# Causal attention by a second score product with keys on the partitions, in place of turned probabilities

## What is computed

```python
q, k = _apply_rope(q, k, cos, sin)          # q, k, v: (8, 16, 512, 8)
scores = jnp.einsum('bhqd,bhkd->bhqk', q, k) / math.sqrt(HEAD_DIM)
scores = scores + jnp.triu(jnp.full((S, S), -jnp.inf), k=1)
probs = jax.nn.softmax(scores, axis=-1)
out = jnp.einsum('bhqk,bhkd->bhqd', probs, v)
return out.transpose(0, 2, 1, 3).reshape(B, S, DIM) @ Wo.T
```

## Time and profile before

| | |
|---|---|
| median of 3 runs | 4396.46 us (4378.6 to 4422.52) |
| the profiled execution | 4409.03 us |
| its span, first to last instruction | 4407.3 us |
| mean granted clock | 0.906 |
| PE, DVE, ACT, POOL busy over the span | 91%, 80%, 58%, 58% |
| last causal mask product starts | 955.7 us |

### The profile page before, as it was taken

The page is one execution under the profiler, slowest core; times in us unless marked ns, Lnnn a source line. Parts: engine busy times, 40 slices in busy tenths (PEclk is TensorE's granted clock), DMA queues, the critical chain, the costliest instruction groups (busy, mean ns, idle before and its releaser), DMA issues. The chain is left out here.

```text
span 4407.3 us, 153325 instructions
## 1 busy us (share of the span) xinstructions
PE 3998.6 (91%) x66018; PEld 2914.3 (66%) x66018; DVE 3520.4 (80%) x5436; ACT 2544.9 (58%) x4654; POOL 2552.0 (58%) x1429
## 2 busy tenths in 40 slices
PE   7899999986998999999999999999999999999996
PEld 4555555545776777777776777777776777777774
DVE  5655555536888889999988898999988889998993
ACT  4544555534555666656656566666665566666563
POOL 2333333326666676667666666667766666666662
PEclk7866666658999999999999999999999999999997
DMA  1000000001211122221211122122121111212112
GB/s 46 4 3 2 2 2 2 3 26 41 54 49 48 48 54 55 53 56 48 62 54 47 49 54 54 52 56 56 48 54 52 51 54 49 56 50 53 50 48 61
DMA packets 122834, 188.19 MB, mean 43 GB/s; under 512 B 24910, under 2 KB 44134, under 8 KB 121964
## 3 DMA queue, kind: packets, MB, share of 16 engines
q1 hardware_dynamic: 122220, 179.07, 15.0%
HBM read 23.78 MB, written 4.19 MB: 6 GB/s over the span
## 5 line engine op out<-in xcount | busy, mean ns | idle before, releaser
L1251 POOL TENSOR_TENSOR rc<-rc,rnorm 128x1024 f32<-128x1024 f32 x384 | 734.5, 1933 | 358.5 <-DVE rnorm L205 358.5
L1245 POOL TENSOR_TENSOR rc<-rc,rs 128x1024 f32<-128x1024 f32 x384 | 905.2, 2369 | 34.5 <-DVE rs L1313 30.8
L1273 POOL TENSOR_TENSOR prob_b<-prob_b,rinv 128x1024 f32<-128x1024 f32 x192 | 365.9, 1906 | 653.0 <-DVE rinv L1386 653.0
L562 POOL TENSOR_TENSOR prob<-prob,rden 128x512 f32<-128x512 f32 (+3 forms) x128 | 297.6, 2325 | 661.3 <-DVE rden L674 661.3
L1307 DVE TENSOR_TENSOR rc<-proj,rope_b 128x1024 f32<-128x1024 f32 x384 | 469.2, 1222 | 114.9 <-PE proj L853 63.8
L941 PE MATMUL ring<-pT,vmoved 64*64 64x32 f32 x18432 | 436.0, 221 | 115.1 <-issue 113.8
L1093 ACT ACTIVATE oT_b<-ring 128x512 f32<-128x512 f32 x384 | 209.6, 596 | 564.6 <-PE ring L941 564.6
L941 PEld LDWEIGHTS ring<-pT,vmoved 64*64 64x64 f32 x18432 | 401.0, 135 | 179.5 <-issue 162.3
L890 PEld LDWEIGHTS ring<-ident,rc 128*128 128x128 f32 x3072 | 362.3, 143 | 235.5 <-POOL rc L1251 77.2
L890 PE MATMUL ring<-ident,rc 128*128 128x128 f32 x3072 | 455.9, 278 | 62.2 <-POOL rc L1251 59.4
L1321 DVE TENSOR_REDUCE sums<-squares 128x16 f32<-128x1024 f32 x384 | 460.2, 1198 | 44.5 <-ACT squares L1105 42.3
(11 more groups left out here) (163 smaller groups left out, 8837.0 us busy)
## 6 DMA issues: line engine op xcount, KB each, us to landing
vmoved<-vown SPq DMA_DIRECT2D x576, 128.0 KB, 2.4
vmoved<-vown SPq DMA_DIRECT2D x192, 192.0 KB, 2.5
vmoved<-vown SPq DMA_DIRECT2D x576, 64.0 KB, 2.1
wqkv_raw<-in_L_ffn_Wqkv SPq DMA_DIRECT2D x40, 192.0 KB, 2.7
wo<-in_L_ffn_Wo SPq DMA_DIRECT2D x6, 512.0 KB, 4.2
x_attended<-xtok SPq DMA_DIRECT2D x8, 256.0 KB, 2.0
xtok_c<-x_attended SPq DMA_DIRECT2D x8, 256.0 KB, 4.4
out<-xtok_c SPq DMA_DIRECT2D x8, 256.0 KB, 2.5
```

Source lines behind the costliest of these rows:

```text
L1245: nc.gpsimd.tensor_tensor(rc[:, k % 2, c, :], rc[:, k % 2, c, :], rs[:, c, :], ALU.add).then_inc(add_done, 1)
L1251: nc.gpsimd.tensor_tensor(dst, dst, rnorm[:, k % 2, c * HEADS:(c + 1) * HEADS].rearrange("p (h o) -> p h o", o=1).broadcast_to([P, HEADS, ...
L1273: nc.gpsimd.tensor_tensor(pr, pr, rinv[:, :, :].rearrange("p q (s o) -> p q s o", o=1).broadcast_to([P, PAIRS, 2, KEYS]), ALU.mult).then_i ...
```

## The change

- The first score product stays, for the maximum alone. Nothing is exponentiated from it.
- The negative maximum of each query, per head, is written to a column of `negmax` and added to a stacked copy of q by PE, as one more row of the contraction (`stack_with_max`: a second stacking of q and four products with the identity). The stacked k gets a row of ones there, by the bias `one` (1 in every 32nd row) as it is copied out. The selection matrices are laid out anew: that row is row 0 of each head's 32, and the parts of q and k take the other places.
- A second score product has the keys on the partitions (`scores_by_key`), one unit being a head and a tile of 128 keys, 512, 384, 256 or 128 queries wide. A second mask `causal_keys` is added to its first 128 columns. Its exponent is the probability, unscaled, already with keys on the partitions, and is written to `probT` by ACT without bias or sum.
- The values get a column of ones, so that row 8 of each head's output strip is the sum. Per group of four heads the output is turned, the reciprocals of the sums taken (DVE), widened to 32 columns (POOL), turned back, and multiplied into the output (DVE).
- Turns of probabilities, their copies, the scaling on POOL and the sum on ACT are gone. Two additions and two subtractions of the rotation per batch move from DVE to POOL.
- The loop over batches is gone: all slots of all batches stand in one row (`A_SLOTS`), with a lag of 24 slots from the first to the second score product, and the steps at fixed slots (`batch_at`, `group_at`). No slot drains at a batch's end.

```diff
-    sel = np.zeros((P, 4, 4, P), f)
+    sel = np.zeros((P, 4, 5, P), f)
...
+            for d in range(A_HDIM):
+                src, dst = A_HDIM * (4 * g + hh) + d, 32 * hh + d
+                for slot, shifts in enumerate(((8, 16), (24,), (8, 24), (16,), (0,))):
+                    for shift in shifts:
+                        sel[src, g, slot, dst + shift] = 1.0
+    out["a_one"] = (np.arange(P) % 32 == 0).astype(f).reshape(P, 1)
...
+PER = 4 * TILES
+LAG = PER + 8
+A_SLOTS = range(-66, NU + 60)
...
+H_AT, Q_AT, QR_AT, K_AT, KR_AT, V_AT = -53, -49, -47, -45, -43, -35
+STACKQ_AT, STACKK_AT, STACK2_AT, TURN_AT, BACK_AT = -24, -22, 18, 46, 52
+Y_AT, YT_AT, H2_AT = 103, 108, 118
...
-        sc = [ps(f"sc{i}", [P, TOKENS]) for i in range(3)]
-        pt = [ps(f"pt{i}", [P, TOKENS]) for i in range(2)]
+        tm = [ps(f"tm{i}", [P, TOKENS]) for i in range(3)]
+        km = [ps(f"km{i}", [P, TOKENS]) for i in range(2)]
...
+            def stack_with_max(gr):
+                bank = begin("stack2", gr)
+                stack(bank, gr, 0, False)
+                pe.wait_ge(max_d, PER * (gr + 1))
+                for j in range(TILES):
+                    last = nc.tensor.matmul(bank[:, j * P:(j + 1) * P], negmax[:, gr % 2, j, :], ident[:, :],
+                                            start=False, stop=(j == TILES - 1))
+                last.then_inc(g_fill, 1)
+
+            def scores(u):
...
+                need(pe, max_d, u - 2)
+                pe.sem_inc(pe_passed, 1)
+                r, g = slice(32 * hh, 32 * hh + 32), gr % GROUPS
+                bank, width = tm[u % 3], (j + 1) * P
+                nc.tensor.matmul(bank[:, 0:width], qkG[r, 0, g, j * P:width], qkG[r, 1, g, 0:width], start=True, stop=False)
+                nc.tensor.matmul(bank[:, j * P:width], ident_bf, causal_mask, start=False, stop=True).then_inc(tm_full, 1)
+
+            def scores_by_key(u):
...
+                need(pe, exp_d, u - 1)
+                pe.sem_inc(pe_passed, 1)
+                r, g = slice(32 * hh, 32 * hh + 32), gr % GROUPS
+                bank, width = km[u % 2], TOKENS - k * P
+                nc.tensor.matmul(bank[:, 0:width], qkG[r, 1, g, k * P:(k + 1) * P], q2[r, gr % 2, k * P:TOKENS],
+                                 start=True, stop=False)
+                nc.tensor.matmul(bank[:, 0:P], ident_bf, causal_keys, start=False, stop=True).then_inc(km_full, 1)
+
+            def weigh(gr, k):
...
+                width = TOKENS - k * P
+                for hh in range(4):
+                    last = nc.tensor.matmul(po[32 * hh:32 * hh + 32, k * P:TOKENS], values[:, b % 2, k, 4 * g + hh, :],
+                                            probT[:, (4 * gr + k) % 3, hh, 0:width], start=(k == 0), stop=True,
+                                            skip_group_check=True)
...
+                gr = group_at(s, TURN_AT)
+                if gr is not None:
+                    bank = begin("turn", gr)
+                    pe.wait_ge(o_out, gr + 1)
+                    four_turns(bank, lambda j: oT[:, gr % 2, j * P:(j + 1) * P])
+                gr = group_at(s, BACK_AT)
+                if gr is not None:
+                    bank = begin("back", gr)
+                    pe.wait_ge(wide_d, gr + 1)
+                    four_turns(bank, lambda j: rden_w[:, gr % 2, j, :, :].rearrange("p h d -> p (h d)"))
...
+                if 0 <= s < NU:
+                    scores(s)
+                if 0 <= s - LAG < NU:
+                    scores_by_key(s - LAG)
+                gr, i = divmod(s - LAG - 6, PER)
+                if i % 4 == 0 and 0 <= gr < NG:
+                    weigh(gr, i // 4)
...
-                        nc.scalar.activation(prob[:, u % RING, i % 4, 0:(j + 1) * P], sc[i % 3][:, 0:(j + 1) * P], ACT.Exp,
-                                             bias=negmax[:, i:i + 1], accum_out=den[:, u % 2, i % 4:i % 4 + 1]).then_inc(e_d, 1)
...
+                    nc.scalar.activation(probT[:, (4 * gr + k) % 3, hh, 0:width], km[u % 2][:, 0:width],
+                                         ACT.Exp).then_inc(exp_d, 1)
...
+                    nc.gpsimd.tensor_copy(rden_w[:, gr % 2, :, :, :], rden[:, gr % 2, :, :].rearrange(
+                        "p t (h o) -> p t h o", o=1).broadcast_to([P, TILES, 4, 32])).then_inc(wide_d, 1)
...
+                    nc.vector.tensor_tensor(oN[:, gr % GROUPS, :], oT[:, gr % 2, :], bank[:, :], ALU.mult).then_inc(g_dve, 1)
```

More of the change, by code:

```diff
@@ L76, in constants @@
     first = bad | ((np.arange(P)[:, None] < WINDOW) & (b < WINDOW))
-    m = np.concatenate([np.where(bad, MASKED, 0.0), np.where(first, MASKED, 0.0), causal, np.eye(P)], 1)
+    m = np.concatenate([np.where(bad, MASKED, 0.0), np.where(first, MASKED, 0.0), causal, causal.T, np.eye(P)], 1)
     out["masks"] = m.astype(mybir.dt.np(mybir.dt.bfloat16))
     return out
[L82 to L111, removed]
 LAST_STEP = NT + 5
@@ L269, in part_a @@
         pe_passed = sem("pe_passed_a")
         block = ctx.enter_context(nc.Block())
[L273 to L306, removed]
+        def gbank(name, k):
+            return gen[GEN[name, k] % 2]
@@ L480, in _, with begin, four_turns @@
-            pipelined(pe, nc.tensor, body)
+            pe.wait_ge(clear_d, 3)
+            def begin(name, k):
+                i = GEN[name, k]
+                if i >= 2:
+                    user = GEN_LIST[i - 2]
+                    if user[0] in BY_VECTOR:
+                        pe.wait_ge(g_dve, GEN_DVE[user] + 1)
+                    else:
+                        pe.wait_ge(g_act, GEN_ACT[user] + 1)
+                return gen[i % 2]
+            def four_turns(bank, src):
+                for j in range(TILES):
+                    last = nc.tensor.transpose(bank[:, j * P:(j + 1) * P], src(j), ident[:, :])
+                last.then_inc(g_fill, 1)
@@ new lines, in project, with value_rows @@
+            def project(name, b, w):
+                bank = begin(name, b)
+                if name == "q":
+                    pe.wait_ge(g_act, GEN_ACT["h", b] + 1)
+                nc.tensor.matmul(bank[:, :], wT[:, w, :], hT[:, :], start=True, stop=True).then_inc(g_fill, 1)
+            def value_rows(b):
+                bank = begin("v", b)
+                for j in range(TILES):
+                    last = nc.tensor.matmul(bank[:, j * P:(j + 1) * P], hT[:, j * P:(j + 1) * P], wT[:, 2, :],
+                                            start=True, stop=True)
+                last.then_inc(g_fill, 1)
@@ new lines, in weigh @@
+            def weigh(gr, k):
+                b, g = divmod(gr, GROUPS)
+                pe.wait_ge(exp_d, PER * gr + 4 * k + 4)
+                if k == 0:
+                    need(pe, o_out, gr)
+                if k == 0 and g == 0:
+                    pe.wait_ge(g_act, GEN_ACT["v", b] + 1)
+                pe.sem_inc(pe_passed, 1)
+                width = TOKENS - k * P
[3 more added lines that the diff above has]
+                                            skip_group_check=True)
+                last.then_inc(w_done, 1)
@@ new lines, in _ @@
+            for s in A_SLOTS:
+                b = batch_at(s, H_AT)
+                if b is not None:
+                    bank = begin("h", b)
+                    pe.wait_ge(nrm, TILES * (NORMS.index(("h", b)) + 1))
+                    four_turns(bank, lambda j: xn[:, j, :])
+                for name, off, w in (("q", Q_AT, 0), ("qr", QR_AT, 4), ("k", K_AT, 1), ("kr", KR_AT, 5)):
+                    if batch_at(s, off) is not None:
+                        project(name, batch_at(s, off), w)
+                if batch_at(s, V_AT) is not None:
+                    value_rows(batch_at(s, V_AT))
+                if group_at(s, STACKQ_AT) is not None:
+                    stack_rows("stackq", group_at(s, STACKQ_AT), 0)
+                if group_at(s, STACKK_AT) is not None:
+                    stack_rows("stackk", group_at(s, STACKK_AT), 1)
+                if group_at(s, STACK2_AT) is not None:
+                    stack_with_max(group_at(s, STACK2_AT))
+                gr = group_at(s, TURN_AT)
[8 more added lines that the diff above has]
+                    four_turns(bank, lambda j: rden_w[:, gr % 2, j, :, :].rearrange("p h d -> p (h d)"))
+                b = batch_at(s, Y_AT)
+                if b is not None:
+                    bank = begin("y", b)
+                    pe.wait_ge(g_dve, GEN_DVE["back", GROUPS * b + GROUPS - 1] + 1)
+                    for g in range(GROUPS):
+                        last = nc.tensor.matmul(bank[:, :], wo_rows[:, g, :], oN[:, g, :], start=(g == 0), stop=(g == GROUPS - 1))
+                    last.then_inc(g_fill, 1)
+                b = batch_at(s, YT_AT)
+                if b is not None:
+                    bank = begin("yt", b)
+                    pe.wait_ge(g_act, GEN_ACT["y", b] + 1)
+                    four_turns(bank, lambda j: yT[:, j * P:(j + 1) * P])
+                b = batch_at(s, H2_AT)
+                if b is not None:
```

(27 more changed lines are left out.)

522 lines of the change are left out of this document (234 added, 288 removed).

## The result

The changed kernel takes 4634.81 us (median of 4, 4633.42 to 4640.85), the kernel before beside it 4409.49: ratio 1.0523, 95% interval 1.0458 to 1.0588. Slower, by 5.2%.

The account below looks back on a forecast made before the run. PE was taken to bound the kernel. Eight batches going from 119.5 to 145.6 us (+209) and +15 once turned 4409.0 us into 4633, stated as 4635; range 4490 to 4810.

Parts of the forecast that it names:

- PE bounds: Causal half: PE, busy 108.9 of 119.4 us a batch, sets the time; other engines matter only through PE's waits.
- The waits: PE's waits in the causal half: some 15 us a batch before the change, falling to 5.
- The price of the second score product: 64 added key-side products with masks per batch: 0.63 to 0.94 us each at 1.2 GHz, +50.2 us (+32 at 2.4).
- case 4: Score weight loads might go under the mask product before, saving 0.2 us on each of 64 products: 4530 us, chance 0.12.
- The clock, 32 us of 2.4 GHz in 145.6: Causal half: PE has 2.4 GHz for 32 us per batch, against 38 before, making the batch 145.6 us.
- turns raise the clock and scores let it fall: PE's clock rises after dense full-array work, turns included, and falls in stretches of 32-row scores; hence 32 us at 2.4 GHz.
- the list: PE's summed prices per batch: 128 us at 1.2 GHz and 72 at 2.4 before the change, 162 and 97 after.
- Weighing at no change: Weighing on PE has fewer, wider products but the same columns, so its change was priced at 0.
- Once per execution, +15: A longer tail before the output product, say 10 us, and more constants to load: +15 us in all.
- The sum 209 + 15: Eight batches of the causal half longer by 145.6 - 119.5 us each, +209, and +15 once: 4409.0 becomes 4633.
- Case 2: PE stays at 2.4 GHz nearly throughout the causal half: a batch of 102 us, 4284 in all; chance 0.12.

Follow-up runs that it names:

- e3: The changed kernel with PE's order in a slot changed: both score products first, then both mask products; 4288.70 us, ratio to the kernel before 0.985.
- e5: The changed kernel with its second score product contracting over all 128 rows instead of the head's own 32; 4158.73 us in one run.
- e4: As e3, with the key side's heads in another order, so a slot's two score products lie on different strips; 4147.57 us, ratio to the kernel before 0.951.
- f1: The changed kernel with four needless f32 turns of the identity ahead of each first score product; 4555.58 us, ratio to the kernel before 1.047.
- f2: The changed kernel with two needless bf16 products of 512 columns ahead of each first score product; 4514.37 us, ratio to the kernel before 1.037.
- e6: The changed kernel without the eight f32 passes that add the negative maximum to the second stacking; 4651.58 us in one run.
- e1: The changed kernel without the mask product on the key side; 4499.35 us in one run.

## Why the prediction was right

- **PE bounds, and what leaves the other engines is worth only its waits.** Shown by the profile after: PE idle 1.9 us in 1160, DVE and POOL down by half and more, time up. The waits fell to 0.2 us a batch where I had 5: that term was set too high.
- **The price of the second score product, 0.63 to 0.94 us at 1.2 GHz.** Measured 0.62, 0.73, 0.83 and 0.94. That most of it is fixed was read from widths; e3 and e5 show what most of it is: the step from a strip of 32 rows to the full array and back. The forecast did not know that. Its case 4 put the loss into the weight load's wait, at 0.12, and this case is out for the changed kernel: with the waits in an instruction of their own the loads still start with their products, as the lines below show. In e4 the second load starts with the first product, once the strips differ.

```profile
879.44 0.28 PEld L430 LDWEIGHTS km<-q,qkG 32*128 32x128 f32 x1
879.44 0.79 PE L430 MATMUL km<-q,qkG 32*128 32x512 f32 x1
```

- **The clock, 32 us of 2.4 GHz in 145.6.** Measured (0.61 - 0.50) / 0.50 x 143.4 = 31.5 us of 143.4. The argument under it, turns raise the clock and scores let it fall, is what f1, f2 and e6 show. That the number met so closely is partly luck: it holds for the last three periods of 143.4 us. The three before them took 138 to 159, and over the 1160 us the mean of 0.58 is a share of 0.16, not 0.22. And e3 shows how near the kernel stands to a much higher clock.
- **Check of the list.** 31.5 / 97 + 111.9 / 162 = 1.02: it explains the batch within 2%.
- **Weighing at no change.** 1.87 against 1.86 us. Right.
- **Once per execution, +15.** The causal half's last copy ends at 1220.2 us, in the kernel before at 981.9: 238 us. Eight times the steady difference, 143.4 - 119.5, is 191. Of the remaining 47 some 22 are the tail (from the start of the last maximum to the end 48 us, before 26) and some 24 slower early batches. The sum 209 + 15 was 14 under as a whole, and its split was off: the eight batches came to 18 us less, the rest to 32 more. The windowed half and the end, which the change does not touch, were 6 us shorter, so the profiled execution, 4640.85, lies 8 over the sum's 4633. In the traces of this case these untouched parts take from 3405 to 3443 us; that the median, 4634.81, met 4635 within a microsecond is luck.
- **Case 2, the high clock, at 0.12.** It did not come, but its mechanism is real and one order away: e3 has it with the same instructions. The forecast priced the fixed part and did not ask whether two products of a slot could share it; that question was worth 346 us (e3) and 487 (e4).

## What to carry to other kernels

Read PE's prices from start to start at both clocks and split them into width and fixed part: here 0.5 of 0.8 us was fixed, and it hung on what stands beside a product, so products on strips of 32 rows belong together, on different strips, with the full-array products behind them. Before PE work is added or removed, ask what it does to the clock: at a mean of 0.6, dense work taken away gained nothing (e6, one run) and wasted work paid (f1, f2). A mean clock is not a share of time: 0.80 is 2.4 GHz for 0.60 of it. And a form should be judged in a good order: as written the changed form loses by 5%, with the order mended it takes 4148 us against 4255 for the kernel before with its products in pairs (ratios 0.951 and 0.977, intervals apart, on two chips). Whether either order is the best for its form was not tried.

## What the runs showed of the hardware that was not expected

- A slot of one 32-row product, a full-array mask, another 32-row product and another mask takes 1.35 us at 1.2 GHz for 128 and 256 columns; with the two products first 1.05, at the same clock.
- Two score products on different strips start in the same instant, weight loads included (403.74 in e4), and a slot of both with both masks takes 0.52 us at 2.4 GHz. They do so unplanned too: taking out one mask between them (e1) made 184 such pairs.
- At 2.4 GHz a key product on a strip starts 0.16 us behind the full-array mask before it, and its mask 0.26 behind it; over all 128 rows these are 0.04 and 0.14 (e5).
- Turns of f32 blocks alone, added to a kernel at a mean clock of 0.58, bring it to 1.00 over 400 us.
- The same instructions in another order move the mean clock of a 400 us stretch from 0.58 to 0.91.
